# Layer norms of a graph attention stage: statistics per tile, or sums over groups of tiles

## The reference, cut to what matters

```python
def _layernorm(x, axis=-1, eps=1e-05):
    m = jnp.mean(x, axis=axis, keepdims=True)
    v = jnp.var(x, axis=axis, keepdims=True)
    return (x - m) / jnp.sqrt(v + eps)
...
# in _L3_gnn_ref: w is the softmax of the edge scores over each node's edges
msg = h[src2] * w[:, :, None]
out = jax.ops.segment_sum(msg, dst2, num_segments=n)
out = out.reshape(n, H * C) + bias
out = out + x
mu = jnp.mean(out, axis=-1, keepdims=True)
var = jnp.var(out, axis=-1, keepdims=True)
out = (out - mu) * jax.lax.rsqrt(var + EPS) * ln_g + ln_b
return out
...
x = _layernorm(x + _L3_gnn_ref(x, edge_index, edge_attr_16, ...), axis=-1)
```

## Time and profile before

| | before |
|---|---|
| median of three runs | 6171.06 us |
| profiled execution, its own time | 6204.05 us |
| span of that execution (first to last instruction) | 6202.3 us |
| VectorE busy | 3342.5 us, 54%, 8895 instructions |
| ScalarE busy | 1718.2 us, 28%, 5753 instructions |
| GpSimd busy | 4463.9 us, 72%, 4570 instructions |
| attention stage | from about 4980 us to the end |

### The profile page before, as it was taken

How to read it: one execution, slowest core, us unless ns; L and a number is a source line. 1 busy time by engine, 2 the same in 40 slices (tenths; PEclk the granted TensorE clock), 3 DMA queues, 4 the chain that set the end, 5 groups by cost and what they waited for, 6 DMA issues and landing times. The chain is left out here.

```text
span 6202.3 us, 54339 instructions
## 1 busy us (share of the span) xinstructions
PE 2518.5 (41%) x12736; PEld 1802.9 (29%) x12736; DVE 3342.5 (54%) x8895; ACT 1718.2 (28%) x5753; POOL 4463.9 (72%) x4570
## 2 busy tenths in 40 slices
PE   6888877567776673000000024656666400000000
PEld 4666656455544452000000012334444300000000
DVE  3333333433444355878778875655555524343666
ACT  1111111211111110333333256777777400000111
POOL 6777777577777766777777437777777777777775
PEclk8777676777899875555555567888788755555555
DMA  4333333866666633222222114333333332222221
GB/s 113 119 116 119 116 118 114 208 210 189 191 188 187 179 94 95 54 54 54 54 54 54 34 47 115 101 112 111 110 111 112 105 98 56 55 56 56 56 53 41
DMA packets 404899, 637.29 MB, mean 103 GB/s; under 512 B 148580, under 2 KB 248966, under 8 KB 404340
## 3 DMA queue, kind: packets, MB, share of 16 engines
q0 software_dynamic: 175664, 424.09, 24.4%
q1 hardware_dynamic: 133028, 112.92, 6.7%
q10 hardware_dynamic: 95904, 96.94, 4.8%
HBM read 529.65 MB, written 103.93 MB: 102 GB/s over the span
## 5 line engine op out<-in xcount | busy, mean ns | idle before, releaser
L1585 POOL DMA_INDIRECT mb_rows<-x_tab,mb_idx x882 | 835.5, 947 | 367.2 <-issue 269.8
L2535 POOL DMA_INDIRECT gt_rows<-h_tab,gt_idx x882 | 842.1, 955 | 307.1 <-issue 273.9
L973 POOL DMA_INDIRECT s_rows<-y_split,srcS x824 | 839.3, 1019 | 292.9 <-issue 233.1
L2035 POOL DMA_INDIRECT eq_ring<-fx_tab,srcS x824 | 834.4, 1013 | 262.3 <-issue 248.2
L555 POOL DMA_INDIRECT s_rows<-in_x,srcS x824 | 784.2, 952 | 273.7 <-issue 247.7
L2070 ACT ACTIVATE eq_ring<-eq_ring 128x64 f32<-128x64 f32 x3328 | 814.5, 333 | 338.6 <-DVE eq_ring L2231 310.7
L2111 PE MATMUL eq_ps<-eq_ring,eq_onehot 128*128 128x320 f32 x1664 | 655.6, 552 | 473.5 <-DVE eq_ring L2231 253.0
L2111 PEld LDWEIGHTS eq_ps<-eq_ring,eq_onehot 128*128 128x128 f32 x1664 | 385.3, 242 | 720.3 <-issue 658.6
L1054 PE MATMUL s_ps<-s_onehot,s_rows 128*128 128x128 bf16 x4992 | 452.0, 247 | 310.0 <-DMA s_rows<-y_split,srcS 300.8
L1695 PE MATMUL mb_ps<-ident,mb_rows 128*128 128x128 f32 x49 | 13.6, 331 | 1282.6 <-ACT mb_rows L1662 1281.3
L629 PE MATMUL s_ps<-s_onehot,s_rows 128*128 128x128 f32 x1664 | 459.7, 393 | 159.6 <-DMA s_rows<-in_x,srcS 152.8
(11 more groups left out here) (503 smaller groups left out, 5693.9 us busy)
## 6 DMA issues: line engine op xcount, KB each, us to landing
w_tab<-s_wrow ACTq DMA_DIRECT2D x208, 264.0 KB
eq_ring<-w_tab SPq DMA_DIRECT2D x208, 264.0 KB, 2.7
s_es<-in_side ACTq DMA_DIRECT2D x208, 136.0 KB
mb_rows<-x_tab,mb_idx POOLq DMA_INDIRECT x882, 2.5
gt_rows<-h_tab,gt_idx POOLq DMA_INDIRECT x882, 2.5
s_rows<-in_x,srcS POOLq DMA_INDIRECT x824
s_rows<-y_split,srcS POOLq DMA_INDIRECT x824
eq_ring<-fx_tab,srcS POOLq DMA_INDIRECT x824
```

The source lines that it names most:

```text
L973: pool.indirect_dma_start(rows[:, n % SLOTS, :], None, t["ys"], bass.IndirectOffsetOnAxis(ap=s["srcS"][:, n:n + 1], axis=0)).then_inc(gath ...
L1585: pool.indirect_dma_start(rows[:, r, n, :], None, t["x1"], bass.IndirectOffsetOnAxis(ap=idx[:, r, n:n + 1], axis=0)).then_inc(gathered[r][ ...
L2035: pool.indirect_dma_start(frow[:, n % SLOTS, :], None, features, bass.IndirectOffsetOnAxis(ap=s["srcS"][:, n:n + 1], axis=0)).then_inc(gat ...
L2535: pool.indirect_dma_start(rows[:, r, n, :], None, flat, bass.IndirectOffsetOnAxis(ap=idx[:, r, n:n + 1], axis=0)).then_inc(gathered[r][g], 16)
```

## The change

The statistics of both closing norms are computed over a whole group at once. The sum is one tensor_reduce over the group in PSUM, followed by a multiply by 1/128; the mean is subtracted in place from the sums in PSUM by one tensor_tensor; ACT squares the centred group in one activation into the buffer that the normalised rows go to afterwards; VectorE reduces the squares in a new function `variance`. The normalising activation no longer has a bias, since its input is centred already. Four semaphores are added (`centred` and `squared`, for each set), and `stats`, `mv` and `less` go.

```diff
@@ -2456,8 +2456,7 @@
         RUNS = -(-TILES // RUN)
         FINISH = [(g, 0, PART[g]) for g in range(NG - 1, 2, -1)] + [(0, 1, slice(0, UPTO[2]))]
         INSIDE = NG - 4
-        stats, mv = sb("stats", [P, 2, MOST, 6]), sb("mv", [P, 2, MOST, 2])
-        var, std, less = sb("var", [P, 2, MOST]), sb("std", [P, 2, MOST]), sb("less", [P, 2, MOST])
+        mean_, var, std = sb("mean", [P, 2, MOST]), sb("var", [P, 2, MOST]), sb("std", [P, 2, MOST])
         spare = s["span_src"][:].rearrange("p t k -> p (t k)").bitcast(F32)
         some = TILES * heads
         ae_sum, ae, alpha, scores, den = (
@@ -2487,9 +2486,10 @@
         gathered = [[sem(f"gathered{r}_{g}") for g in range(NG)] for r in range(2)]
         consumed = [[sem(f"consumed{r}_{c}") for c in range(RUNS)] for r in range(2)]
         scattered = sem("scattered")
-        under_ready, powers_ready, var_ready, std_ready, ln_ready, normed = (
-            [sem(f"{n}{e}") for e in range(2)] for n in ("under_ready", "powers_ready", "var_ready", "std_ready", "ln_ready", "normed"))
-        per_span = [*idx_ready, below_ready, ex_ready, r_copied, r_landed, *under_ready, *powers_ready, *var_ready, *std_ready,
+        under_ready, powers_ready, centred, squared, var_ready, std_ready, ln_ready, normed = (
+            [sem(f"{n}{e}") for e in range(2)] for n in ("under_ready", "powers_ready", "centred", "squared", "var_ready",
+                                                         "std_ready", "ln_ready", "normed"))
+        per_span = [*idx_ready, below_ready, ex_ready, r_copied, r_landed, *under_ready, *powers_ready, *centred, *squared, *var_ready, *std_ready,
                     *ln_ready, *normed]
         block = ctx.enter_context(nc.Block(no_gpsimd_drain=True))
 
@@ -2563,6 +2563,9 @@
             def rooted(k, l):
                 g, e, mine = FINISH[k]
                 many = mine.stop - mine.start
+                act.wait_ge(centred[e], l + 1 if e else 2 * k + l + 1)
+                act.activation(rows[:, 1 - l, mine, 0:D], sums_of[e][:, 0:many * D].rearrange("p (u d) -> p u d", d=D),
+                               ACT.Square).then_inc(squared[e], 1)
                 act.wait_ge(var_ready[e], l + 1 if e else 2 * k + l + 1)
                 act.activation(std[:, e, 0:many], var[:, e, 0:many], ACT.Sqrt).then_inc(std_ready[e], 1)
 
@@ -2570,8 +2573,8 @@
                 g, e, mine = FINISH[k]
                 act.wait_ge(ln_ready[e], l + 1 if e else 2 * k + l + 1)
                 for u in range(mine.stop - mine.start):
-                    last = act.activation(rows[:, 1 - l, mine.start + u, 0:D], sums_of[e][:, u * D:(u + 1) * D], ACT.Identity,
-                                          bias=less[:, e, u:u + 1], scale=std[:, e, u:u + 1])
+                    last = act.activation(rows[:, 1 - l, mine.start + u, 0:D], sums_of[e][:, u * D:(u + 1) * D], ACT.Copy,
+                                          scale=std[:, e, u:u + 1])
                 last.then_inc(normed[e], 1)
 
             def finish(*those):
@@ -2687,16 +2690,21 @@
                 do(dve.tensor_tensor(under[e][:, 1, 0:many], x, z, ALU.subtract))
                 dve.sem_inc(under_ready[e], 1)
 
-            def spread(do, k):
+            def spread(do, k, l):
                 g, e, mine = FINISH[k]
                 many = mine.stop - mine.start
-                for u in range(many):
-                    do.put(dve.bn_stats(stats[:, e, u], sums_of[e][:, u * D:(u + 1) * D]))
-                do.sync()
-                for u in range(many):
-                    do.put(dve.bn_aggr(mv[:, e, u], stats[:, e, u]))
-                do.sync()
-                dve.tensor_scalar(var[:, e, 0:many], mv[:, e, 0:many, 1], 1e-5, None, ALU.add).then_inc(var_ready[e], 1)
+                sums = sums_of[e][:, 0:many * D].rearrange("p (u d) -> p u d", d=D)
+                mean = mean_[:, e, 0:many]
+                do(dve.tensor_reduce(mean, sums, AX_X, ALU.add))
+                do(dve.tensor_scalar(mean, mean, 1.0 / D, None, ALU.mult))
+                dve.tensor_tensor(sums, sums, mean.unsqueeze(2).broadcast_to([P, many, D]), ALU.subtract).then_inc(centred[e], 1)
+
+            def variance(do, k, l):
+                g, e, mine = FINISH[k]
+                many = mine.stop - mine.start
+                dve.wait_ge(squared[e], l + 1 if e else 2 * k + l + 1)
+                do(dve.tensor_reduce(var[:, e, 0:many], rows[:, 1 - l, mine, 0:D], AX_X, ALU.add))
+                dve.tensor_scalar(var[:, e, 0:many], var[:, e, 0:many], 1.0 / D, 1e-5, ALU.mult, ALU.add).then_inc(var_ready[e], 1)
 
             def join(do, k):
                 g, e, mine = FINISH[k]
@@ -2718,14 +2726,13 @@
                                      ALU.mult))
                 do(dve.tensor_tensor(sums, sums, own_part, ALU.add))
                 do(dve.tensor_tensor(sums, sums, own_row[:, mine, HW:HR], ALU.add))
-                spread(do, k)
+                spread(do, k, 0)
 
             def scale_of(do, k, l):
                 g, e, mine = FINISH[k]
                 many = mine.stop - mine.start
                 dve.wait_ge(std_ready[e], l + 1 if e else 2 * k + l + 1)
                 do(dve.reciprocal(std[:, e, 0:many], std[:, e, 0:many]))
-                do(dve.scalar_tensor_tensor(less[:, e, 0:many], mv[:, e, 0:many, 0], -1.0, std[:, e, 0:many], ALU.mult, ALU.mult))
                 dve.sem_inc(ln_ready[e], 1)
 
             def again(do, k):
@@ -2737,7 +2744,7 @@
                 dve.wait_ge(normed[e], 1 if e else 2 * k + 1)
                 do(dve.tensor_tensor(sums, rows[:, 1, mine, 0:D], row(gain_row), ALU.mult))
                 do(dve.tensor_tensor(sums, sums, rows[:, 0, mine, 0:D], ALU.add))
-                spread(do, k)
+                spread(do, k, 1)
 
             def finish(*those):
                 dve.sem_clear(end)
@@ -2747,9 +2754,13 @@
                 for k in those:
                     join(do, k)
                 for k in those:
+                    variance(do, k, 0)
+                for k in those:
                     scale_of(do, k, 0)
                 for k in those:
                     again(do, k)
+                for k in those:
+                    variance(do, k, 1)
                 for k in those:
                     scale_of(do, k, 1)
 
```

## The result

In one comparison of eleven runs each, the changed kernel took 6191.7 us in the median (6178.77 to 6201.24) and the kernel before 6176.18 (6164.53 to 6183.11): ratio **1.0022, 95% interval 1.0014 to 1.0031**. That is about 13.6 us slower (8.6 to 19), where +13.7 was forecast. The profiled execution of the changed kernel happened to be shorter than that of before (span 6180.2 us against 6202.3): the difference lies ahead of the attention stage, and two spans alone would have told the opposite of the truth.

A forecast was written before the change was run, and what follows sets the result against it. The chain of waits was taken to be led by POOL's indirect gathers, with part of the closing work on the path; 4.7 + 8.7 + 0.3 = +13.7 us gave 6184.8 us, range 6171 to 6204 (8 in 10).

The forecast's parts named there:

- Hidden finishes: The finishes of 6, 7 and 9 tiles during the sweep: VectorE's idle after them hides all their added time, 0.
- VectorE's own loss at nine tiles: In a nine-tile finish during the sweep: VectorE alone loses some 5 us.
- 10-tile finish: Fourth finish in the sweep: each of two norms takes 2.36 us longer, +4.7 us, counted whole to the end.
- the Copy: ACT's normalising without bias: 0.299 us per tile against Identity's 0.36, a gain of 0.06 us per tile.
- Last finish: Closing finish of 8 and 9 tiles together: VectorE's planning starts 8.7 us late, Square queued behind Sqrt.
- a sign of being right: In the last finish: the planning comes 8 to 9 us later.
- the hand-overs: Passing work between VectorE and ACT within a finish, priced at 0.05 us each.
- Clearing: SyncE clears four more semaphores before POOL's restart, about 0.08 us each, +0.3 us.
- No change that can be told: Whole kernel: 0.22% slower, under the about 0.3% (18.5 us) taken as what a measurement can tell.
- a slow reduction out of PSUM: Rival, chance 0.18: reductions from PSUM are slower than from SBUF, 17.7 or 20.9 us in all.
- a hidden 10-tile finish: Rival, chance 0.14: later POOL and VectorE slack takes up the 4.7 us, only 9.0 us stay.
- more table loads: Rival, chance 0.06: Square needs its own ACT set, up to 10 us more on the path, 23.9 in all.

The follow-up runs named there:

- first-three kernel: The kernel before with only the first three finishes (6, 7 and 9 tiles) taking the new norms; ratio to before 1.0005 (0.9996 to 1.0014).
- the repeated reduction: The changed kernel with the 9-tile finish's first reduction repeated six times more; 1033.29 us to the 10-tile finish, 3.8 more than the changed kernel.

## Why the prediction was right

- *Hidden finishes, 0*: right. Shown by the first-three kernel, and the depth of the cover by the repeated reduction. VectorE's own loss at nine tiles, put at some 5 us, was 3.7.
- *10-tile finish, +4.7*: measured +4.0 (31.17 - 27.13), carried to the end in full. The term that was too large is the Copy: ten took 2.69 us, not 2.99, since out of PSUM one takes about 0.27 us and not the 0.299 read where the source was SBUF. The other steps of a norm came within 0.06 us in sum.
- *Last finish, +8.7*: measured from its first Exp to the planning 36.08 before and 43.62 after, +7.5, just short of the 8 to 9 that the prediction named as a sign of being right. The mechanism was there as described, Square behind Sqrt included. Too large were the hand-overs (no gap before the first Copy, and Square overlapping Sqrt's end: 7.34 instead of 7.78, and 7.79 instead of 8.1 in the second norm) and again the Copies.
- *Clearing, +0.3*: from the planning's last instruction to POOL's restart 3.17 us before, 3.39 after: +0.2. The planning itself was 0.2 shorter, so the sum of the stretch is 7.56.
- Together the stretches give +11.9 us (4.04 + 0.35 + 7.56 - 0.05), inside the timed 8.6 to 19; the 0.35 is within what that stretch varies by. The forecast of 13.7 was some 2 too large by them: the mechanism was right, and the median's 13.6 is not evidence for the last 2 us.
- *"No change that can be told"*: too cautious. With eleven runs of each the interval of 1.0014 to 1.0031 leaves out 1, so 0.22% was told, where the prediction took 0.3% as the least.
- *The rivals*: a slow reduction out of PSUM fell to the 1491 ns; a hidden 10-tile finish to the stretch of 93.55; more table loads to their count. Where its input is ready, the activation behind a load starts at once: in the 6-tile finish of the changed kernel the load ends at 5728.14 and the Sqrt starts at 5728.15. The Trainium skill (ScalarE: Activation LUTs, What ACT_TABLE_LOAD costs) puts a drain of some 1.38 us on each switch besides; no such drain is seen here.

```profile
5726.86 1.28 ACT L2570 ACT_TABLE_LOAD   x1
5728.15 0.21 ACT L2570 ACTIVATE gt_std<-gt_var 128x6 f32<-128x6 f32 x1
```

## What to carry to other kernels

Fewer instructions is not less time: ten bn_stats and bn_aggr read a tile once and took 2.85 us, while two whole-group reductions alone take 2.98, and the centring and the squares come on top, each waiting for the one before. Before pricing an edit that stands in several places, read what each place is followed by: here three of five cost nothing, up to the idle that follows, and two cost every microsecond. The idle of the engine that gets the work is not the whole of it: with the squares on VectorE its cover held, and POOL's gathers were late all the same. Where two engines take turns over two sets of data, issue on the helping engine first what is ready (both Squares), and only then what waits.

## What was not expected

Copy with a per-partition scale ran faster out of PSUM (17 in 4.49 us, 0.264 each) than out of SBUF (14 in 4.18 us, 0.299 each). Within the 10-tile finish the kernel with the squares on VectorE shows the same: ten Copies out of SBUF took 3.03 us, out of PSUM 2.69.
